# Normalising between the stages of a transformer kernel: ScalarE scales, chunks are turned one by one, some statistics, splits and waits stand elsewhere

## What is computed

```python
def _layernorm(x, axis=-1, eps=1e-05):
    m = jnp.mean(x, axis=axis, keepdims=True)
    v = jnp.var(x, axis=axis, keepdims=True)
    return (x - m) / jnp.sqrt(v + eps)

x = L0_attn_hidden_states                            # (2, 1024, 128)
x = x + _L0_attn_ref(_layernorm(x, axis=-1), ...)    # causal softmax attention, power-law mask, 16 heads of 8
x = x + _L0_ffn_ref(_layernorm(x, axis=-1), ...)     # (silu(x wg) * (x wu)) wd, 384 hidden, integer weights / 127
x = x + _L1_attn_ref(_layernorm(x, axis=-1), ...)    # rotary q and k, softmax-one over the first axis (of 2)
x = x + _L1_ffn_ref(_layernorm(x, axis=-1), ...)     # base + shared low-rank + top 2 of 6 low-rank experts
x = x + _L2_attn_ref(_layernorm(x, axis=-1), ...)    # causal linear attention, elu + 1
x = x + _L2_ffn_ref(_layernorm(x, axis=-1), ...)     # top 2 of 8 gelu experts, a layernorm behind each
x = x + _L3_attn_ref(_layernorm(x, axis=-1), ...)    # random-feature attention, relu features, 16 heads
x = x + _L3_ffn_ref(_layernorm(x, axis=-1), ...)     # top 2 of 8 gated experts, threshold routing
```

## Time and profile before

| | |
|---|---|
| median of 3 timed runs | 1104.17 us |
| lowest and highest | 1096.57 and 1106.09 us |
| profiled execution, its own time | 1102.42 us |
| span of its profile | 1100.3 us |
| mean granted clock of TensorE | 0.887 of full |
| busy: PE, PEld (weight loads) | 896.0 us (81%), 606.8 us (55%) |
| busy: DVE, ACT, POOL | 665.8 us (61%), 427.8 us (39%), 512.2 us (47%) |

### The profile page before, as it was taken

How to read it: one execution, slowest core, us unless ns; L and a number is a source line. 1 busy time by engine, 2 the same in 40 slices (tenths; PEclk the granted TensorE clock), 3 DMA queues, 4 the chain that set the end, 5 groups by cost and what they waited for, 6 DMA issues and landing times. The chain is left out here.

```text
span 1100.3 us, 17965 instructions
## 1 busy us (share of the span) xinstructions
PE 896.0 (81%) x6334; PEld 606.8 (55%) x6334; DVE 665.8 (61%) x1876; ACT 427.8 (39%) x1024; POOL 512.2 (47%) x463
## 2 busy tenths in 40 slices
PE   4668999999999867267899699994998987389992
PEld 2122333333333356155566588994895756389982
DVE  6767778686872075879687656778003666533334
ACT  2323665565666441113111276774334211032220
POOL 5425888888898831053222344555200001156661
PEclk9657999899999988758799799997999998599997
DMA  4800110110000000001000000302000001266764
GB/s 146 257 1 1 31 31 2 30 30 19 13 2 24 1 22 8 0 15 40 1 2 1 10 21 10 134 9 77 1 1 1 1 10 30 89 188 216 217 196 145
DMA packets 38893, 55.95 MB, mean 51 GB/s; under 512 B 6954, under 2 KB 26290, under 8 KB 38678
## 3 DMA queue, kind: packets, MB, share of 16 engines
q1 hardware_dynamic: 36310, 49.70, 14.9%
q0 software_dynamic: 2496, 5.12, 1.6%
HBM read 43.66 MB, written 10.94 MB: 50 GB/s over the span
## 5 line engine op out<-in xcount | busy, mean ns | idle before, releaser
L423 POOL TENSOR_TENSOR arena<-arena 128x1024 f32<-128x1024 f32 (+3 forms) x105 | 201.0, 1946 | 42.4 <-ACT arena L598 42.3
L665 DVE CUSTOM_DVE_ANT_0 ps<-ps,arena 128x512 f32<-128x512 f32 (+3 forms) x256 | 148.7, 640 | 45.3 <-PE ps L480 44.4
L598 ACT ACTIVATE arena<-ps 128x512 f32<-128x512 f32 (+3 forms) x320 | 137.3, 491 | 89.4 <-PE ps L511 58.1
L480 PE MATMUL ps<-arena 48*128 48x512 bf16 (+3 forms) x384 | 103.9, 371 | 24.9 <-DVE arena L665 15.9
L117 POOL TENSOR_SCALAR vareps<-meanvar 128x4 f32<-128x4 f32 x32 | 7.9, 246 | 213.2 <-DVE meanvar L98 213.2
L503 PE MATMUL ps<-arena 51*128 51x512 bf16 (+3 forms) x384 | 76.0, 349 | 6.0 <-DMA arena<-arena 5.2
L2075 PE MATMUL ps<-arena 128*128 128x128 f32 x624 | 79.9, 284 | 0.0
L480 PEld LDWEIGHTS ps<-arena 48*128 48x128 bf16 x384 | 28.3, 95 | 91.3 <-DVE arena L665 55.1
L2075 PEld LDWEIGHTS ps<-arena 128*128 128x128 f32 x624 | 76.4, 200 | 0.0
L152 PE MATMUL ps<-ident,xn 128*128 128x128 f32 x128 | 26.0, 352 | 59.4 <-DVE x L921 19.9
L532 PE MATMUL ps<-arena 128*9 128x512 f32 (+3 forms) x640 | 67.7, 495 | 3.9 <-POOL arena L423 3.9
(11 more groups left out here) (341 smaller groups left out, 2081.0 us busy)
## 6 DMA issues: line engine op xcount, KB each, us to landing
arena<-in_L_ffn_w SPq DMA_DIRECT2D x39, 512.0 KB, 3.7
arena<-scratch SPq DMA_DIRECT2D x32, 192.0 KB, 4.0
arena<-in_L_ffn_w SPq DMA_DIRECT2D x16, 256.0 KB, 3.4
scratch<-arena SPq DMA_DIRECT2D x12, 256.0 KB, 4.4
arena<-expert_rows SPq DMA_DIRECT2D x8, 256.0 KB, 4.9
scratch<-arena SPq DMA_DIRECT2D x4, 384.0 KB, 5.0
scratch<-arena SPq DMA_DIRECT2D x12, 128.0 KB, 4.3
...
```

Of the source, the lines that this page charges most:

```text
L423: nc.gpsimd.tensor_tensor(e, e, weight[:, at:at + k].unsqueeze(1).broadcast_to([P, 2, k]), ALU.mult).then_inc(weighed, 1)
L480: nc.tensor.matmul(m.ps[:, (2 * k + e) % MAX_BANKS, 0:wd], qs[rows, u % BUFS, pair, i * P:(i + 1) * P], ks[rows, u % BUFS, pair, first:fir ...
L598: nc.scalar.activation(probs(g)[:, 2 * p + e, 0:wd], m.ps[:, BANK[h, e], 0:wd], ACT.Exp, scale=SCALE).then_inc(exps, 1)
L665: nc.vector.tensor_tensor_reduce(out=scores, in0=scores, in1=before[:, 0:wd], scale=-1.0, scalar=negrest[:, h, i:i + 1] if i < TPC else 3e ...
```

## The change

1. **Normalising moves from VectorE to ScalarE.** `normalise` becomes `scale`: ACTIVATE with function Identity, `bias` = a column `shift` and `scale` = a column `rstd`, both one value per partition. GpSimd now also makes `shift` = -mean * rstd, in two small operations per chunk (the negation ahead of the power, the product behind it). `after` on VectorE is statistics alone.
2. **When ScalarE scales.** `copy_xnT` scales up to `lookahead[n]` chunks in front of the copy of chunk n: (3, 3, 4, 4) as a rule, (2, 3, 4, 4) in `l0_attn`, (2, 2, 3, 4) in `l1_ffn`, (1, 2, 3, 4) in `l3_attn`, (3, 3, 3, 4) in `l3_ffn`.
3. **When TensorE turns.** The wait for the last chunk's add is now a table, `turn_after`; it stays at `l0_attn`, `l0_ffn`, `l2_attn` and `l2_ffn` and is gone at `l1_attn`, `l1_ffn`, `l3_attn` and `l3_ffn`, where a chunk is turned once it is scaled.
4. **`l0_ffn`**: statistics of chunks 0 and 1 stand behind the last three hidden products, those of chunk 2 ahead of the last add.
5. **`l1_attn`**: the widening is ScalarE's, with the scaling of chunks 0 and 1 behind it, ahead of the copies of the rotated weights.
6. **`l2_ffn`**: the gate products wait for `xnT` alone, the low parts are waited for by the first expert's up products; the low part of the first expert's weights stands on GpSimd behind the low part of chunk 0 instead of behind all of them; the last chunk's statistics come at the start of `l3_attn`, behind its low products.
7. **`l3_attn`**: the cast of the constant moves behind the normalising work; TensorE waits for the add of the chunk before behind its first two spreads instead of ahead of them; at its end the statistics of chunk c - 2 stand ahead of the add of chunk c - 1.
8. **`l3_ffn`**: the logits lie in PSUM bank 0 instead of 5.

```diff
@@ class Norm
+        self.lookahead, self.turn_after, self.behind_low = (3, 3, 4, 4), {0: [before.ready[NC - 1]]}, {}
     def after(self, dve, c):
         self.statistics(dve, c)
-        if c and self.early:
-            self.normalise(dve, c - 1)
     def vector(self, dve):
         while self.counted_stats < NC:
             self.statistics(dve, self.counted_stats)
-        while self.counted_xn < NC:
-            self.normalise(dve, self.counted_xn)
-    def normalise(self, dve, c):
+    def scale(self, act, c):
         nc, m = self.nc, self.m
         self.counted_xn += 1
-        dve.wait_ge(m.ln_rstd, 2 * self.value(c))
+        act.wait_ge(m.ln_rstd, 4 * self.value(c))
         for t in range(c * TPC, (c + 1) * TPC):
-            last = nc.vector.tensor_scalar(m.xn[:, t, :], m.x[:, t, :], m.meanvar[:, t, 0:1],
-                                           m.rstd[:, t:t + 1], ALU.subtract, ALU.mult)
+            last = nc.scalar.activation(m.xn[:, t, :], m.x[:, t, :], ACT.Identity, bias=m.shift[:, t:t + 1], scale=m.rstd[:, t:t + 1])
         last.then_inc(m.ln_xn, 1)
     def gpsimd(self, pool, bias):
             nc.gpsimd.tensor_scalar(m.vareps[:, ts], m.meanvar[:, ts, 1], LN_EPS, None, ALU.add).then_inc(m.ln_rstd, 1)
-            pool.wait_ge(m.ln_rstd, 2 * self.value(c) - 1)
+            nc.gpsimd.tensor_scalar(m.shift[:, ts], m.meanvar[:, ts, 0], -1.0, None, ALU.mult).then_inc(m.ln_rstd, 1)
+            pool.wait_ge(m.ln_rstd, 4 * self.value(c) - 2)
             nc.gpsimd.tensor_tensor(m.rstd[:, ts], m.vareps[:, ts], m.power[:, ts], ALU.pow).then_inc(m.ln_rstd, 1)
+            pool.wait_ge(m.ln_rstd, 4 * self.value(c) - 1)
+            nc.gpsimd.tensor_tensor(m.shift[:, ts], m.shift[:, ts], m.rstd[:, ts], ALU.mult).then_inc(m.ln_rstd, 1)
@@ wait_xnT
-        if self.turned == 0:
-            pe.wait_ge(*self.before.ready[NC - 1])
         while self.turned < min(c + 2, NC):
             n = self.turned
+            for over in self.turn_after.get(n, []):
+                pe.wait_ge(*over)
             pe.wait_ge(m.ln_xn, self.value(n))
@@ copy_xnT
             n = self.copied
+            while self.counted_xn < self.lookahead[n]:
+                self.scale(act, self.counted_xn)
             act.wait_ge(m.ln_turned, self.value(n))
@@ l0_ffn vector
             nc.vector.tensor_tensor(xs, m.ps[:, 4 + c % 2, :].rearrange("p (j d) -> p j d", d=D), xs, ALU.add).then_inc(x_done, 1)
-            after(dve, c)
...
+            if c == NC - 1:
+                for k in range(c - 1):
+                    after(dve, k)
             if c:
                 add(c - 1)
+        after(dve, NC - 2)
         add(NC - 1)
+        after(dve, NC - 1)
@@ l1_attn
+    def widen(act):
+        act.wait_ge(w_in, w_all)
         for j in range(2):
-            ins = nc.vector.tensor_copy(bwide[:, j, :], bcol[:, j:j + 1].broadcast_to([P, P]))
+            ins = nc.scalar.activation(bwide[:, j, :], bcol[:, j:j + 1].broadcast_to([P, P]), ACT.Copy)
         ins.then_inc(widened, 1)
+        for c in range(2):
+            norm.scale(act, c)
@@ l2_ffn
-                norm.wait_xnT(pe, t // TPC)
+                norm.wait_xnT(pe, t // TPC, parted=False)
...
+            if e == 0:
+                norm.wait_parts(pe, c)
...
+    norm.behind_low = {0: lambda pool: split_weights(pool, 0)}
@@ l3_attn
-            if c:
-                pe.wait_ge(x_done, norm.done(c - 1))
             for r in range(RT + 1):
                 if r < RT:
                     spread(c, r)
+                if r == 1 and c:
+                    pe.wait_ge(x_done, norm.done(c - 1))
...
+            if c >= 2:
+                after(dve, c - 2)
             if c:
                 add(c - 1)
+        after(dve, NC - 1)
```

54 lines of the change are left out of this document (33 added, 21 removed).

## The result

The changed kernel takes 1093.82 us, the median of 10 runs (1088.75 to 1096.44); the kernel before 1103.68 us, the median of 10 (1095.57 to 1114.87). The ratio is 0.9926, with a 95% interval of 0.9897 to 0.9955: faster by 0.7%, and 0.8 us from the forecast of 1093. The profiled execution of the changed kernel took 1089.5 us.

A forecast was written before the change was run, and what follows sets the result against it. No engine is busy throughout; chains over several engines end each stage, so the change acts at the seven seams and the start. Terms summed to -9.5 us from the profiled 1102.4, giving 1093 us, range 1090 to 1097 (chance 0.50).

The forecast's parts named there:

- The price of a chunk: Normalising on ScalarE: four 128x128 ACTIVATEs with two per-partition operands, 1.18 or 1.46 us, taken as 1.5 us a chunk.
- Start, +0.8: Kernel start: ScalarE scales chunk 3 before copying chunk 2, so the copy and TensorE's resumption come later, +0.8 us.
- First feed-forward, +1.0 and -1.8: First feed-forward: TensorE waits behind chunk 3's scaling, +1.0 us; VectorE's product in chunk 3 is no longer held, -1.8 us.
- the first rival: Whole kernel: ScalarE's chunk costs less (1.18 us) or the clock helps (2 to 3 us); 1086 to 1090 us, chance 0.25.
- End of the first feed-forward, -3.3 behind the add: Seam into the second attention: widening done early on ScalarE, rotation follows at once, first projection starts sooner, -3.3 us.
- Inside the second attention, -1.0: Second attention: the normalising of chunk 0 leaves VectorE's chain, -1.0 us.
- Its end, -1.7: Second attention's end: a turning, copy and product per chunk after the last add; last product read earlier, -2.7 with the -1.0.
- Third attention to third feed-forward, -3.35: Third feed-forward's start: gate products wait only for the copy, not GpSimd's low part; logits read 3.35 us earlier.
- Fourth attention, -2.2 and +2.9: Fourth attention's end: the stall before the last chunk's outputs goes, -2.2 us; late statistics and copies delay the logits, +2.9 us.
- Third feed-forward to fourth attention, -0.6: Fourth attention's start: TensorE starts 2.3 us earlier, but two turnings wait 0.85 us each for ScalarE's scaling; net -0.6 us.
- the third: Rival, whole kernel: ScalarE is the wrong engine, its chunks before awaited copies cost more than VectorE's; 1114 us, chance 0.04.
- The fourth: Rival, all seams: turning still waits for the last add and copies for ScalarE, so lengths stay; 1102 us, chance 0.04.

The follow-up runs named there:

- the second profile of before: The kernel before, unchanged, profiled once more to see what repeats: 1115.45 us, taken in a slower clock state.
- scal_only: Changed kernel with only the normalising's move to ScalarE (items 1 and 2), items 3 to 8 undone: 1097.86 us, ratio 1.0002 to the kernel before.
- vec_norm: Changed kernel with normalising back on VectorE, all placements kept: 1087.64 us, ratio 0.9904 to the kernel before.
- undo_turn: Changed kernel with all eight starts waiting for the last add before the first turning: no total given; stretches read 26.60 and 13.59 us.

## Why the prediction was right, and where it was not

The time (1093.8 for 1093) and the direction were right, and so was the place of the largest single gain, the gate products' wait. But that the sum came out so close is luck: its errors cancelled, and the lower clock behind a wait, which was worth 1.5 us and more at several seams, had no term in the sum.

- **The price of a chunk.** 1.5 us forecast; four ACTIVATEs take 1.63 to 1.65 us, 482 ns each and 390 ns apart, everywhere, and none is slowed by GpSimd. The 128x128 form with two operands is 0.18 us over the plain one, so 0.09 us an operand and not 0.07. The Trainium skill ("ScalarE: Activation LUTs", what ACT_TABLE_LOAD costs) gives 93 ns an operand; the trace agrees, and so it does with the estimate of 1.64 us a chunk worked out from that figure. GpSimd's two operations cost 0.6 us a chunk on the way to the scale, not 0.45, and from the end of an add to GpSimd's start it is 1.41 us in the earlier trace rows, not 1.3.
- **Start, +0.8.** Wrong: the copy of chunk 2 came at 20.75 us, 0.3 later than before, since ScalarE was free a microsecond sooner than I had it, and the resumption (33.00) hangs on the landed parts alone.
- **First feed-forward, +1.0 and -1.8.** Against the first profile of before the terms are +3.1 and -3.6, and their sum of -0.55 near the forecast -0.8 is luck; against the second they are +2.9 and -2.0. The waits were right: 1.1 us more at the first place, 1.9 us fewer at the second. Left out was the fall of the clock behind the first (1.6 us). The fall at the second, from which the first rival promised 2 to 3 us, was not tied to the wait: the second profile of before has the same wait and no fall.
- **End of the first feed-forward, -3.3 behind the add.** Only -1.4 between the first profiles (-2.3 between the second). The first projection came 5.11 us behind the last add against 8.02 before, 2.9 us sooner where 3.3 were forecast, but 1.5 us were lost at the lower clock right behind it. The part that I had named, the widening, is not what decides: undone, it moves the first projection by 1.2 us only, while the statistics' place moves it by 1.5 us the other way, and without any of the placed parts it stands 4.3 us later. Which of them brings those 4.3 us was not tested singly.
- **Inside the second attention, -1.0.** Right: -0.96, in every profile of a kernel without VectorE's normalising there.
- **Its end, -1.7.** Only -0.2. I had counted a turning, a copy and one product for each chunk. But the product of chunk 2 stands on TensorE behind the turning of chunk 3, so two products (3.15 us) follow the last copy.
- **Third attention to third feed-forward, -3.35.** Right, and too small: -4.2, with +0.5 given back behind it; the part for which it was claimed brings 3.8.
- **Fourth attention, -2.2 and +2.9.** The first exact (-2.26), the second +4.2 and +5.5. The first copy stands 3.6 us behind the last add's start, 3.4 by my sum; what I had wrong is the way from there to the logits, 8.8 and 10.0 us instead of 7.6, because the gate products ran at the lower clock behind 3.35 us of waiting. So the two rows together are +2.0 and +3.2 where +0.7 was forecast.
- **Third feed-forward to fourth attention, -0.6.** The two waits of 0.9 us inside it were there (0.86 both). The stretch is -0.4 in the first pair, but of six further profiles of the same program four took 101.5 us, 1.1 more than before, and two 100.3 and 100.4: not confirmed.
- **Chance.** From the second row to the last logits, the first two profiles show -5.2 us, not the 12.6 of their spans. The timed ratios (0.9926 and 0.9938, so 8.2 and 6.8 us) lie between the 5.2 and the forecast of 9.5.

The rivals: ScalarE's chunk stayed far from the 2.3 us at which the gain would be gone, though `scal_only` and `vec_norm` bear out the third in part: ScalarE gains nothing over VectorE. The fourth was partly true: in `undo_turn` early turning changes nothing at either of the seams read. The fall of the clock behind a wait, the term that the sum lacked, was worth 1.5 to 1.6 us at each of two places.
